# A four-layer transformer kernel: router scatters one step sooner, normalising ahead of the batch chains, clearing at step 0, expert weights ahead of rows

## The chip, the cores and the metric

The kernel is one program on one core of a Trainium2 chip. The metric is the time of one execution on the device, in microseconds. An effect below about 0.2% of it can't be told from no change.

## The reference

8192 tokens (128 sequences of 64) of width 128 go through four layers, each an attention to a context and a feed-forward part, both behind a layer norm and a gate:

```python
x = x + tanh(g_xattn[i]) * xattn_i(layernorm(x), ctx)
x = x + tanh(g_ffn[i]) * ffn_i(layernorm(x))
```

- Attention: 16 heads. Layer 0 has a key width of 64 per head (1024 in all), layers 1 to 3 of 8 (128 in all). Layer 2 has a mask, layer 3 uses stablemax in place of softmax.
- Feed-forward of layers 0 and 3: a top-1 mixture of 8 experts with a capacity of 1024 tokens each. `logits = x @ W`, the expert is the argmax, and a token's place in its expert is the running count of the tokens ahead of it that chose the same (`cumsum(onehot) - 1`); tokens past the capacity are dropped. The rows of each expert go through `act(X @ W1 + b1) @ W2 + b2`, 128 to 512 to 128.
- Feed-forward of layer 1: two quantised linear maps.
- Feed-forward of layer 2: a top-2 mixture of 8 experts, `silu(x @ Wg) * (x @ Wu) @ Wd`, without a capacity.

## The kernel before

Each engine (PE for matmuls, DVE for vectors, ACT for activations, POOL, and SP for DMAs) has its own program and runs in order; semaphores tie them. The code of an engine is a loop of steps; in step `t` an engine does stage `s` of item `t - s`, so that all stages of different items overlap. The program has these parts in a row: attention of layer 0 (`attention_wide`, one tile of 128 tokens per step, 64 steps), experts of layer 0, attention of layer 1 with its quantised feed-forward behind it in the same loop, attention of layer 2 (`attention_split`, two tiles per step, 32 steps), the middle experts, attention of layer 3 (`attention_split`), the last experts. In the trace the three `attention_split` are told apart by time; their tiles all have names with `l_`.

**The router.** The class `Router` (in the loops called `tail`) hangs behind the attention of layers 0, 2 and 3. For each item that the attention has finished it does, in stages counted from `T0` (8 in layer 0):

- DVE (`Router.dve`): `bn_stats` (L702), `bn_aggr` (L754) of the same item, and one step later `tensor_scalar` L759, which writes the normalised rows `xn` from the mean and from `rstd`.
- POOL: `add_eps` (L624, waits for the aggregate) and `root` (L629, a power), which give `rstd`.
- PE and ACT: transpose of the rows (L653), scores (L661). DVE copies the scores (L670).
- Per batch of `nb` steps two short chains of dependent small operations on DVE: the **choice** chain (L726 to L749), which picks the expert by maximum and comparison and writes `chosen`; PE counts who is ahead (L642 to L646); the **slots** chain (L709 to L719), which turns the counts into the row number `put` of each token. `nb` is 4 in layers 0 and 3 and 2 in layer 2. A step with the first chain is called a choice step below, one with the second a slots step. In layer 3 the slots step comes right behind the choice step.
- POOL (`Router.scatter`, L617): one indirect DMA per tile and choice writes the rows to `slots` in memory at the places `put`. That is 1 per step in layer 0, 4 in layer 2, 2 in layer 3. The first of a step waits for `put_done` and for the landing of the scatters of two steps before. The item that is sent in step `t` is that of stage `s + 4 + nb`: one step behind the one in which the slots chain of its batch runs.

**POOL's order.** In layer 0 a step is: attention's norms, `scatter`, `add_eps`, `root`. In layer 2 (`folded`): wait for `scored`, `scatter`, then L916 (epsilon for the attention's norm), L624, L921 (its power), L629. In layer 3 (`stable`): L916, L624, L921, L629, then `Head.combine` (L397 twice, L401, L403: the results of the middle experts are weighted and added to x), then a wait for `o_filled`, then `scatter`. POOL's aggregate of step `t` is that of DVE's step before.

**DVE's order in `attention_split`**, after L1026 and L670 of the step: L991 (`l_xn`, waits for POOL's L921), L978 and L982 (statistics of a later item; in layer 3 L978 waits for L403), L1039 and L1041 (context divided, which PE L1298 waits for), L966 (x updated), `Router.dve`, L1061 (a 128x1024 product). `prepare` (L950) clears `l_val`, `l_split`, `l_recip` and the router's tiles; PE's first L1239 waits for it (`ready`).

**Experts.** `experts` handles items of 512 rows. For the middle ones (`dynamic`) the row numbers and the expert of an item are read from tables. SP issues per step the rows of item `t` (L1789, two DMAs) and the first weights of item `t - 1` (L1797, two DMAs); PE transposes the rows (L1976) and multiplies (L1968).

Of the kernel before, what the change touches and what calls it, by code (L numbers as in the profile page):

```python
# [7 lines left out]
ALU = mybir.AluOpType  # L8
# [520 lines left out]
class Router:  # L529
# [58 lines left out]
    def depth(self):  # L588

        return 5 + self.nb  # L590
# [8 lines left out]
    def scatter(self, nc, pool, t, s):  # L599

        g, k = self.g, self.tiles
        out = s + 4 + self.nb
        sent_before = t.landed(out + 2, k * self.ks)

        slotted = t.batches(out - self.nb + 1 + (t.t - out) % self.nb, self.nb) if t.live(out) else None
        if t.live(out):

            if self.slots_clear and t.t == out:

                pool.wait_ge(*self.slots_clear)  # L610
            for tile in range(t.item(out) * k, t.item(out) * k + k):
                for c in range(self.ks):

                    if c == 0 and tile % k == 0:
                        wait(pool, self.put_done, slotted)
                        wait(pool, self.sent[t.par(out)], sent_before)
                    pool.indirect_dma_start(  # L617
                        self.slots, bass.IndirectOffsetOnAxis(ap=g.put[c][:, tile:tile + 1], axis=0), g.row[:, tile, self.sent_cols], None,
                        bounds_check=self.slots.shape[0] - 1, oob_is_err=False).then_inc(self.sent[t.par(out)], 16)
# [56 lines left out]
    def dve(self, nc, dve, t, s, updated, n_updated, read, n_read):  # L676
# [21 lines left out]
        if t.live(s):  # L698
# [4 lines left out]
            last.then_inc(self.part, 1)  # L703
        if batch4:
# [46 lines left out]
        if t.live(s):  # L751
            wait(dve, self.part, n0)
            for tile in range(k):
                last = V.bn_aggr(self.mv[:, t.par(s), tile, :], self.st[:, t.par(s), tile, :])  # L754
            last.then_inc(self.stats, 1)
        if t.live(s + 1):
            wait(dve, self.rstd_done, n1)
            for tile in range(k):
                last = V.tensor_scalar(  # L759
                    g.xn[:, t.item(s + 1) * k + tile, :], g.x[:, t.item(s + 1) * k + tile, :],  # L760
                    self.mv[:, t.par(s + 1), tile, 0:1], self.rstd[:, t.par(s + 1), tile:tile + 1], ALU.subtract, ALU.mult)
            last.then_inc(self.xn_done, 1)
# [16 lines left out]
def attention_split(nc, g, name, gate_col, kind, head=None, stream=None, router=None, together=None, weights=None, out=None, follow=None):  # L779
# [13 lines left out]
    with ExitStack() as ctx:  # L793
# [113 lines left out]
        def _(pool):  # L907
            def step(t):
                if folded:

                    wait(pool, scored, t.done(SCORE))
                    tail.scatter(nc, pool, t, T0)
# [15 lines left out]
                if stable:  # L928

                    wait(pool, o_filled, t.done(OUT))  # L930
                    tail.scatter(nc, pool, t, T0)
# [16 lines left out]
        def _(dve):  # L948
# [121 lines left out]
            for t in range(FOLLOW + follower.STEPS if follower else STEPS):  # L1070
                if t == 3:
# [294 lines left out]
def attention_wide(nc, g, t_in, router, dropped, later):  # L1366
# [7 lines left out]
    with ExitStack() as ctx:  # L1374
# [88 lines left out]
        def _(pool):  # L1463
            def step(t):
# [14 lines left out]
                tail.scatter(nc, pool, t, 8)  # L1479
                tail.add_eps(nc, pool, t, 8)  # L1480
                tail.root(nc, pool, t, 8)

# [219 lines left out]
def experts(nc, g, name, slots, rows, w1, b1, w2, b2, kind, gate_col, last=False, early=None):  # L1702
# [13 lines left out]
    with ExitStack() as ctx:  # L1716
# [55 lines left out]
        def _(sp):  # L1772
            def step(t):
# [8 lines left out]
                if t.live(0):  # L1782

                    wait(sp, xt_filled, n4)
# [6 lines left out]
                if t.live(1):  # L1791

                    wait(sp, h_filled[3], t.done(1 + WS))
                    if not dynamic:
                        wait(sp, h_drained[3], n3)
                    for h in range(HALVES):
                        sp.dma_start(w1_s[:, t.par(1, WS), h, :, :], at(w1_v, expert(sp, t, 1, h))).then_inc(w1_in[t.par(1, WS)], 16)  # L1797
                    if not dynamic:
                        sp.dma_start(b1_s[:, t.par(1), :], b1[bass.ds(expert(sp, t, 1, 0), 1)].rearrange("a f c -> (a f) c")).then_inc(
                            w1_in[t.par(1, WS)], 16)  # L1800
# [530 lines left out]
```

## Time and profile before

| | us |
|---|---|
| median of 3 runs | 2513.36 |
| lowest, highest | 2510.45, 2514.68 |
| the profiled execution | 2513.01 |
| its span | 2511.2 |

The span runs from the first to the last instruction; 1.8 us lie around it. The granted TensorE clock was 0.915 of full speed on the mean. Busy time of the engines by stage, in us:

| stage | from, to | PE | DVE | ACT | POOL |
|---|---|---|---|---|---|
| layer 0 attention | 0, 780 | 716 | 559 | 400 | 284 |
| layer 0 experts | 780, 922 | 125 | 70 | 42 | 68 |
| layer 1 | 922, 1375 | 354 | 373 | 368 | 184 |
| layer 2 attention | 1375, 1795 | 348 | 328 | 192 | 183 |
| middle experts | 1795, 2025 | 209 | 119 | 46 | 141 |
| layer 3 attention | 2025, 2368 | 273 | 274 | 261 | 237 |
| last experts | 2368, 2511 | 123 | 64 | 43 | 62 |

Over the span PE is busy 2146.8 us (85%), DVE 1787.9 (71%), ACT 1350.6 (54%), POOL 1157.7 (46%). DMA issues are not counted as busy time of SP. A busy engine in the table isn't a bound by itself: what counts is which one the others wait for, and that is read from the idle time in brackets at the end of a row in the timeline and from the releaser named beside it.

### The profile page before, as it was taken

What the parts mean: (1) busy time and instruction counts of PE and PEld (TensorE: products, weight loads), DVE (VectorE), ACT (ScalarE), POOL (GpSimd) and SP (SyncE); (2) the same over time, 40 slices, a digit from 0 to 9 for tenths busy, and PEclk for the clock granted to TensorE, in tenths of its full rate; (3) what the DMA queues carried; (4) which work ended last, traced back from release to release, by engine and by line L of the source; (5) the groups of instructions that cost most, each with busy time, mean ns of one, the idle gap of its engine ahead of it and who ended that gap; (6) DMA issues with size and microseconds to landing.
All of it is one profiled execution on the core that took longest, in us unless ns stands there. A gap on an engine that the chain in (4) does not pass through costs nothing. (4 is left out here: it accounts for less than half of the span.)

```text
span 2511.2 us, 81208 instructions
## 1 busy us (share of the span) xinstructions
PE 2146.8 (85%) x33432; PEld 1717.8 (68%) x33443; DVE 1787.9 (71%) x5105; ACT 1350.6 (54%) x2499; POOL 1157.7 (46%) x1712
## 2 busy tenths in 40 slices
PE   6999999999995969999555799998399958898597
PEld 5887878787874746777444577776399947777375
DVE  3777777777773648887896589886555559988354
ACT  3555555555551327886998455553122259979232
POOL 1333333434343541113776125555466666876444
PEclk8999999999997979998677899997699979989699
DMA  6330000000005621110000111111487622332363
GB/s 194 110 123 27 25 27 25 24 21 20 20 18 152 180 85 55 55 58 17 1 1 3 32 37 52 52 51 36 134 235 230 185 75 79 106 96 79 101 185 103
DMA packets 225233, 195.14 MB, mean 78 GB/s; under 512 B 34444, under 2 KB 197846, under 8 KB 224864
## 3 DMA queue, kind: packets, MB, share of 16 engines
q1 hardware_dynamic: 186336, 143.52, 19.6%
q0 software_dynamic: 18944, 36.98, 4.2%
q10 hardware_dynamic: 19584, 9.44, 1.3%
q8 instruction: 265, 4.34, 0.8%
q14 instruction: 104, 0.85, 0.1%
HBM read 113.53 MB, written 70.55 MB: 73 GB/s over the span
## 5 line engine op out<-in xcount | busy, mean ns | idle before, releaser
L617 POOL DMA_INDIRECT slots<-row,put x256 | 258.1, 1008 | 211.5 <-issue 131.2
L1968 PE MATMUL experts_H<-experts_xs_t,experts_w 128*128 128x256 f32 (+1 forms) x832 | 253.5, 456 | 9.9 <-DMA experts_w<-in_F_w 4.7
L1102 ACT ACTIVATE l_prob_t<-l_banks 128x512 f32<-128x512 f32 x256 | 132.2, 603 | 145.9 <-PE l_banks L1219 115.4
L1968 PEld LDWEIGHTS experts_H<-experts_xs_t,experts_w 128*128 128x128 f32 x832 | 156.7, 195 | 74.5 <-issue 54.0
L1474 POOL TENSOR_TENSOR l_var_eps<-l_mv,eps 128x1 f32<-128x1 f32 x64 | 12.1, 189 | 413.9 <-DVE l_mv L1555 413.9
L1277 PE MATMUL l_banks<-l_val,l_prob_t 128*64 128x18 f32 x5120 | 201.1, 215 | 0.0
L1277 PEld LDWEIGHTS l_banks<-l_val,l_prob_t 128*64 128x64 f32 x5120 | 190.3, 143 | 8.1 <-issue 0.7
L1510 DVE TENSOR_REDUCE l_top<-l_S 128x16 f32<-128x1024 f32 x64 | 78.3, 1224 | 161.7 <-PE l_S L1653 161.7
L1986 PE MATMUL experts_Y<-experts_w,experts_hid 128*128 128x128 f32 x1600 | 190.0, 275 | 3.5 <-DVE experts_y L1912 2.6
L1986 PEld LDWEIGHTS experts_Y<-experts_w,experts_hid 128*128 128x128 f32 x1600 | 184.3, 192 | 5.0 <-issue 4.9
L1823 POOL DMA_INDIRECT rows<-experts_y,experts_idx x144 | 139.9, 971 | 90.0 <-DVE experts_y L1908 52.9
L1012 DVE TENSOR_REDUCE l_top<-l_banks 128x32 f32<-128x2048 f32 x64 | 146.5, 2288 | 46.3 <-PE l_banks L1226 33.7
L916 POOL TENSOR_TENSOR l_var_eps<-l_mv,eps 128x2 f32<-128x2 f32 x96 | 24.3, 253 | 302.3 <-DVE l_mv L982 218.7
L1944 ACT ACTIVATE experts_hid<-experts_H,experts_b_scaled 128x512 f32<-128x512 f32 x128 | 80.0, 687 | 135.2 <-DVE experts_b_scaled L1864 115.7
L1619 PE MATMUL l_R<-l_ctx_t,l_wk 128*128 128x128 f32 x1024 | 134.2, 286 | 11.6 <-DMA l_ctx_t<-in_ctx_t 11.6
L1619 PEld LDWEIGHTS l_R<-l_ctx_t,l_wk 128*128 128x128 f32 x1024 | 122.5, 196 | 19.9 <-issue 18.3
L1469 POOL TENSOR_TENSOR l_prob<-l_prob,l_recip 128x1024 f32<-128x1024 f32 x64 | 121.3, 1895 | 24.6 <-DVE l_recip L1506 24.6
L1941 ACT ACTIVATE experts_act_gate<-experts_H 128x512 f32<-128x512 f32 x72 | 43.0, 597 | 163.3 <-PE experts_H L1968 163.3
L1567 ACT ACTIVATE l_q_t<-l_R 128x512 f32<-128x512 f32 x128 | 76.4, 597 | 96.9 <-PE l_R L1619 96.9
L1619 PE MATMUL l_R<-l_xn_t,l_wq 128*128 128x128 f32 x1024 | 126.5, 277 | 2.0 <-DVE l_xn_t L1527 2.0
L1690 PE MATMUL l_R<-l_wo,l_out_t 128*64 128x128 f32 x2048 | 126.1, 276 | 0.0
L1111 ACT ACTIVATE l_k_m<-l_banks,early_bk_masked,const_table 128x256 f32<-128x256 f32 x256 | 124.9, 595 | 0.0
(312 smaller groups left out, 5943.4 us busy)
## 6 DMA issues: line engine op xcount, KB each, us to landing
experts_w<-in_F_w SPq DMA_DIRECT2D x136, 256.0 KB
l_ctx_t<-in_ctx_t SPq DMA_DIRECT2D x96, 128.0 KB, 2.4
early_q_m<-l_q_t SPq DMA_DIRECT2D x384, 32.0 KB, 1.8
experts_xs<-slots SPq DMA_DIRECT2D x72, 132.0 KB
experts_w<-in_F_w ACTq DMA_DIRECT2D x72, 128.0 KB, 3.3
slots<-l_empty SPq DMA_DIRECT2D x16, 536.0 KB, 4.1
experts_xs<-slots SPq DMA_DIRECT2D x16, 536.0 KB
slots<-l_empty SPq DMA_DIRECT2D x16, 520.0 KB, 5.9
```

Source lines behind the costliest of these rows:

```text
L617: pool.indirect_dma_start(self.slots, bass.IndirectOffsetOnAxis(ap=g.put[c][:, tile:tile + 1], axis=0), g.row[:, tile, self.sent_cols], No ...
L1012: V.tensor_reduce(top[:, :, :].rearrange("p r a -> p (r a)"), X[:, :, :].rearrange("p r (a k) -> p (r a) k", k=64), AX.X, ALU.max).then_in ...
L1102: nc.scalar.activation(prob_t[:, t.par(PROB), r, :], Z[:, r, :], ACT.Exp).then_inc(prob_done, 1)
L1111: last = nc.scalar.activation(k_m[:, t.par(PROJ, SLOTS_QK), j, :], QK[:, 256:512], ACT.Identity, bias=bk_masked[:, j:j + 1], scale=g.const ...
L1277: last = nc.tensor.matmul(O[64 * tile:64 * tile + 64, 18 * h:18 * h + 18], term[:, t.par(OUT), h // 4, col:col + 64], val[:, t.par(OUT), t ...
L1469: nc.gpsimd.tensor_tensor(prob[:, t.par(5, 4), :, :, :], prob[:, t.par(5, 4), :, :, :], recip[:, t.par(5), :, :].unsqueeze(3).broadcast_to ...
L1619: last = nc.tensor.matmul(R[:, BANK[name], P * k:P * k + P], w[:, 4 * (c % 2) + k, :], moving, start=True, stop=True)
L1690: last = nc.tensor.matmul(MISC[64 * b:64 * b + 64, P:2 * P], out_t[:, t.par(7), k, b, :], wo_s[:, b, k, :], start=k == 0, stop=k == 7)
L1823: pool.indirect_dma_start(rows, bass.IndirectOffsetOnAxis(ap=idx[:, t.par(4, XS), k:k + 1], axis=0), y[:, t.par(4), k, :], None, bounds_ch ...
L1944: nc.scalar.activation(hid[:, t.par(2), c, :], H[:, c, :], ACT.Gelu if kind == "gelu" else ACT.Relu, bias=b1_scaled[:, t.par(2), c:c + 1], ...
L1968: last = nc.tensor.matmul(H[:, c, cols], w1_s[:, t.par(2, WS), h, c, :], xs_t[:, t.par(2), cols], start=True, stop=True)
L1986: last = nc.tensor.matmul(Y[:, P * k:P * k + P], hid[:, t.par(3), c, P * k:P * k + P], w2_s[:, t.par(3, WS), k // SUBS, c, :], start=c == ...
```

## The change

There are five edits.

1. `Router.depth` is `4 + nb` instead of `5 + nb`, and `scatter` sends the item of stage `s + 3 + nb` instead of `s + 4 + nb`, in layers 0, 2 and 3. The first item of a batch goes out in the step of its slots chain.
2. In `Router.dve`, L759 (now L707) and L754 (now L714) stand ahead of the slots chain and the choice chain, the normalising first.
3. In `attention_wide`, POOL's `scatter` stands behind `add_eps` and `root`; in layer 2 it stands at the end of POOL's step, with its wait for `scored`.
4. In `attention_split`, `prepare` runs at step 0 of DVE's loop instead of step 3, in layers 1, 2 and 3.
5. For the middle experts SP issues in step `t` the first weights of item `t`, then its rows. The weights' wait (`h_filled[3]` of four items before) now stands ahead of the rows. The other experts keep their order.

```diff
     def depth(self):
 
-        return 5 + self.nb
+        return 4 + self.nb
...
     def scatter(self, nc, pool, t, s):
 
         g, k = self.g, self.tiles
-        out = s + 4 + self.nb
+        out = s + 3 + self.nb
...
             last.then_inc(self.part, 1)
+        if t.live(s + 1):
+            wait(dve, self.rstd_done, n1)
+            for tile in range(k):
+                last = V.tensor_scalar(
+                    g.xn[:, t.item(s + 1) * k + tile, :], g.x[:, t.item(s + 1) * k + tile, :],
+                    self.mv[:, t.par(s + 1), tile, 0:1], self.rstd[:, t.par(s + 1), tile:tile + 1], ALU.subtract, ALU.mult)
+            last.then_inc(self.xn_done, 1)
+        if t.live(s):
+            wait(dve, self.part, n0)
+            for tile in range(k):
+                last = V.bn_aggr(self.mv[:, t.par(s), tile, :], self.st[:, t.par(s), tile, :])
+            last.then_inc(self.stats, 1)
         if batch4:
...
             last.then_inc(self.chosen_done, 1)
-        if t.live(s):
-            wait(dve, self.part, n0)
...
-            last.then_inc(self.stats, 1)
-        if t.live(s + 1):
-            wait(dve, self.rstd_done, n1)
...
-            last.then_inc(self.xn_done, 1)
...
             def step(t):
-                if folded:
-
-                    wait(pool, scored, t.done(SCORE))
-                    tail.scatter(nc, pool, t, T0)
                 if t.live(NORM):
...
                     wait(pool, o_filled, t.done(OUT))
                     tail.scatter(nc, pool, t, T0)
+                if folded:
+
+                    wait(pool, scored, t.done(SCORE))
+                    tail.scatter(nc, pool, t, T0)
...
-                if t == 3:
+                if t == 0:
                     prepare()
                     dve.wait_ge(ready, 1)
...
-                tail.scatter(nc, pool, t, 8)
                 tail.add_eps(nc, pool, t, 8)
                 tail.root(nc, pool, t, 8)
+                tail.scatter(nc, pool, t, 8)
...
+            def load_w1(t, s):
+
+                wait(sp, h_filled[3], t.done(s + WS))
+                for h in range(HALVES):
+                    sp.dma_start(w1_s[:, t.par(s, WS), h, :, :], at(w1_v, expert(sp, t, s, h))).then_inc(w1_in[t.par(s, WS)], 16)
+
...
                 if t.live(0):
 
+                    if dynamic:
+                        load_w1(t, 0)
                     wait(sp, xt_filled, n4)
...
-                if t.live(1):
-
-                    wait(sp, h_filled[3], t.done(1 + WS))
-                    if not dynamic:
-                        wait(sp, h_drained[3], n3)
-                    for h in range(HALVES):
-                        sp.dma_start(w1_s[:, t.par(1, WS), h, :, :], at(w1_v, expert(sp, t, 1, h))).then_inc(w1_in[t.par(1, WS)], 16)
...
+                if t.live(1) and not dynamic:
+                    wait(sp, h_drained[3], n3)
+                    load_w1(t, 1)
```

DVE, layer 3, a slots step, before (L702 and L754 are the router's statistics, L712 to L719 the chain that writes `put`, L759 the normalising, L1061 the attention's next work):

```order
3465 L702 BN_STATS l_tail_st<-row 128x6 x2
3466 L712 TENSOR_TENSOR l_cand<-l_hot,l_counts 128x64
3467 L713 TENSOR_REDUCE l_rank<-l_cand 128x8
3468 L716 TENSOR_SCALAR l_lost<-l_rank 128x8
3469 L717 TENSOR_TENSOR l_slot<-l_rank,l_expert_base 128x8
3470 L718 TENSOR_TENSOR l_rank<-l_slot,l_lost 128x8
3471 L719 CAST put<-l_rank 128x8
3472 L754 BN_AGGR l_tail_mv<-l_tail_st 128x2 x2
3473 L759 TENSOR_SCALAR row<-row,l_tail_mv,l_tail_rstd 128x128 x2
3474 L1061 TENSOR_TENSOR l_soft<-l_soft,l_prob_t 128x1024
```

and the same place in the changed kernel:

```order
3465 L702 BN_STATS l_tail_st<-row 128x6 x2
3466 L707 TENSOR_SCALAR row<-row,l_tail_mv,l_tail_rstd 128x128 x2
3467 L714 BN_AGGR l_tail_mv<-l_tail_st 128x2 x2
3468 L724 TENSOR_TENSOR l_cand<-l_hot,l_counts 128x64
3469 L725 TENSOR_REDUCE l_rank<-l_cand 128x8
3470 L728 TENSOR_SCALAR l_lost<-l_rank 128x8
3471 L729 TENSOR_TENSOR l_slot<-l_rank,l_expert_base 128x8
3472 L730 TENSOR_TENSOR l_rank<-l_slot,l_lost 128x8
3473 L731 CAST put<-l_rank 128x8
3474 L1061 TENSOR_TENSOR l_soft<-l_soft,l_prob_t 128x1024
```

The normalising and the aggregate moved ahead of the six rows of the chain; `put` is written two rows (four instructions) later. L1061 stays behind both.

POOL, layer 3, the place of the first scatters, before:

```order
1122 L403 TENSOR_TENSOR row<-row,l_term 128x2x128
1123 L916 TENSOR_TENSOR l_var_eps<-l_mv,eps 128x2
1124 L624 TENSOR_TENSOR l_tail_var_eps<-l_tail_mv,eps 128x2
1125 L921 TENSOR_TENSOR l_rstd<-l_var_eps,neg_half 128x2
1126 L629 TENSOR_TENSOR l_tail_rstd<-l_tail_var_eps,neg_half 128x2
1127 L397 TENSOR_TENSOR l_term<-l_got,weight 128x256 x2
1128 L401 TENSOR_TENSOR l_term<-l_term 128x256
1129 L403 TENSOR_TENSOR row<-row,l_term 128x2x128
1130 L617 DMA slots<-row,put 8192x268 x2
```

and in the changed kernel:

```order
1122 L403 TENSOR_TENSOR row<-row,l_term 128x2x128
1123 L617 DMA slots<-row,put 8192x268 x2
1124 L912 TENSOR_TENSOR l_var_eps<-l_mv,eps 128x2
1125 L624 TENSOR_TENSOR l_tail_var_eps<-l_tail_mv,eps 128x2
1126 L917 TENSOR_TENSOR l_rstd<-l_var_eps,neg_half 128x2
1127 L629 TENSOR_TENSOR l_tail_rstd<-l_tail_var_eps,neg_half 128x2
```

The first pair of a batch now stands one step sooner, ahead of the next step's norms and combine. In layer 2 POOL's rows stand in the same order in both kernels; what they wait for differs.

SP, the start of the middle experts, before (each DMA behind the load of its table entry):

```order
453 L1778 TENSOR_LOAD tile_row
...
456 L1789 DMA experts_xs<-slots 128x2x132
...
460 L1789 DMA experts_xs<-slots 128x2x132
...
464 L1789 DMA experts_xs<-slots 128x2x132
...
468 L1789 DMA experts_xs<-slots 128x2x132
...
472 L1797 DMA experts_w<-in_F_w 128x512
...
476 L1797 DMA experts_w<-in_F_w 128x512
```

and in the changed kernel:

```order
453 L1758 TENSOR_LOAD tile_expert
...
456 L1777 DMA experts_w<-in_F_w 128x512
...
460 L1777 DMA experts_w<-in_F_w 128x512
...
464 L1797 DMA experts_xs<-slots 128x2x132
...
468 L1797 DMA experts_xs<-slots 128x2x132
...
472 L1777 DMA experts_w<-in_F_w 128x512
...
476 L1777 DMA experts_w<-in_F_w 128x512
```

The weights of item 0 moved ahead of all rows, and those of item 1 ahead of the rows of item 1.

## Rows read from the trace of the kernel before

Of a row of the timeline: start in us, duration in us, engine, line, operation, output and inputs by name, and in brackets the idle time of the engine before it and what ended it.

**Rows 1.** Timeline, end of layer 0's attention: start us, us, engine, line, operation, [idle before]

```profile
764.58 0.45 PE L653 MATMUL l_R<-const_table,row 128*128 128x128 f32 x1 [2.27 <-DVE row L759]
```

**Rows 2.** Timeline, the first steps of layers 1, 2 and 3

```profile
924.99 0.37 ACT L1122 COPY l_xn_t<-l_banks 128x256 f32<-128x256 f32 x1 [21.73 <-PE l_banks L1253]
926.70 1.22 PE L1239 MATMUL l_banks<-l_ctx_t,early_wk 128*128 128x256 f32 x2 [1.75 <-DVE l_recip L957]
...
1382.12 0.54 DVE L953 MEMSET l_val<- 64x576 f32 x1
1382.84 0.37 ACT L1122 COPY l_xn_t<-l_banks 128x256 f32<-128x256 f32 x1 [5.43 <-PE l_banks L1253]
1383.87 1.22 PE L1239 MATMUL l_banks<-l_ctx_t,early_wk 128*128 128x256 f32 x2 [1.07 <-DVE l_recip L957]
...
2034.21 1.22 PE L1239 MATMUL l_banks<-l_ctx_t,early_wk 128*128 128x256 f32 x2 [3.31 <-DVE l_recip L957]
```

**Rows 3.** Timeline, one batch of layer 2 in full flow

```profile
1575.25 0.17 DVE L719 CAST put<-l_rank 128x4 uint32<-128x4 f32 x1
...
1576.28 1.04 POOL L617 DMA_INDIRECT slots<-row,put  x1 [5.65 <-issue]
...
1581.45 0.73 POOL L921 TENSOR_TENSOR l_rstd<-l_var_eps,neg_half 128x2 f32<-128x2 f32 x1
...
1584.47 0.59 DVE L991 TENSOR_SCALAR l_xn<-row,l_mv,l_rstd 128x128 f32<-128x128 f32 x2
```

**Rows 4.** Timeline, end of layer 2's attention

```profile
1755.89 0.60 DVE L759 TENSOR_SCALAR row<-row,l_tail_mv,l_tail_rstd 128x128 f32<-128x128 f32 x2 [1.69 <-POOL l_tail_rstd L629]
1756.04 1.10 POOL L617 DMA_INDIRECT slots<-row,put  x1 [0.19 <-issue]
...
1769.38 0.19 DVE L709 TENSOR_TENSOR l_ranked<-l_counts,l_slot_base 128x32 f32<-128x32 f32 x1
...
1770.23 0.96 POOL L617 DMA_INDIRECT slots<-row,put  x1 [1.86 <-issue]
...
1770.57 0.17 DVE L719 CAST put<-l_rank 128x4 uint32<-128x4 f32 x1
...
1788.48 0.97 POOL L617 DMA_INDIRECT slots<-row,put  x1 [0.30 <-issue]
```

**Rows 5.** Timeline, start of the middle experts

```profile
1791.94 3.88 SPq L1789 DMA_DIRECT2D experts_xs<-slots  x4
...
1796.59 1.46 SPq L1797 DMA_DIRECT2D experts_w<-in_F_w  x2
...
1801.28 1.19 PE L1968 MATMUL experts_H<-experts_xs_t,experts_w 128*128 128x256 f32 x2 [4.67 <-DMA experts_w<-in_F_w]
```

**Rows 6.** Timeline, layer 3: a choice step, the slots step behind it, a later step

```profile
2153.82 0.21 POOL L624 TENSOR_TENSOR l_tail_var_eps<-l_tail_mv,eps 128x2 f32<-128x2 f32 x1 [1.23 <-DVE l_tail_mv L754]
...
2157.89 1.57 DVE L991 TENSOR_SCALAR l_xn<-row,l_mv,l_rstd 128x128 f32<-128x128 f32 x2
...
2159.54 1.06 POOL L617 DMA_INDIRECT slots<-row,put  x1 [0.17 <-issue]
...
2162.67 0.17 DVE L719 CAST put<-l_rank 128x8 uint32<-128x8 f32 x1
...
2163.24 1.96 POOL L921 TENSOR_TENSOR l_rstd<-l_var_eps,neg_half 128x2 f32<-128x2 f32 x1
2163.40 1.22 DVE L1061 TENSOR_TENSOR l_soft<-l_soft,l_prob_t 128x1024 f32<-128x1024 f32 x1
...
2168.01 0.72 POOL L403 TENSOR_TENSOR row<-row,l_term 128x256 f32<-128x256 f32 x1
2168.77 0.49 DVE L978 BATCH_NORM_STATS2 l_st<-row 128x6 f32<-128x128 f32 x2 [0.75 <-POOL row L403]
...
2247.79 1.06 POOL L617 DMA_INDIRECT slots<-row,put  x1 [5.52 <-PE l_banks L1277]
```

**Rows 7.** Timeline, end of layer 3's attention

```profile
2355.03 0.97 POOL L617 DMA_INDIRECT slots<-row,put  x1 [0.30 <-issue]
```

More of the change, by code:

```diff
@@ L750, in dve @@
             last.then_inc(self.chosen_done, 1)
-        if t.live(s):
-            wait(dve, self.part, n0)
-            for tile in range(k):
-                last = V.bn_aggr(self.mv[:, t.par(s), tile, :], self.st[:, t.par(s), tile, :])
-            last.then_inc(self.stats, 1)
-        if t.live(s + 1):
-            wait(dve, self.rstd_done, n1)
[L758 to L761, printed above, removed]
-            last.then_inc(self.xn_done, 1)
     def chain(self, count, name):
@@ L1790, in step @@
                             x_in[t.par(0, XS)], 16)
-                if t.live(1):
-                    wait(sp, h_filled[3], t.done(1 + WS))
-                    if not dynamic:
-                        wait(sp, h_drained[3], n3)
-                    for h in range(HALVES):
-                        sp.dma_start(w1_s[:, t.par(1, WS), h, :, :], at(w1_v, expert(sp, t, 1, h))).then_inc(w1_in[t.par(1, WS)], 16)
-                    if not dynamic:
-                        sp.dma_start(b1_s[:, t.par(1), :], b1[bass.ds(expert(sp, t, 1, 0), 1)].rearrange("a f c -> (a f) c")).then_inc(
-                            w1_in[t.par(1, WS)], 16)
+                if t.live(1) and not dynamic:
+                    wait(sp, h_drained[3], n3)
+                    load_w1(t, 1)
+                    sp.dma_start(b1_s[:, t.par(1), :], b1[bass.ds(expert(sp, t, 1, 0), 1)].rearrange("a f c -> (a f) c")).then_inc(
+                        w1_in[t.par(1, WS)], 16)
                 if t.live(2) and not dynamic:
```

## Prediction

> **What bounds the kernel now.** The table of stages in the section on time and profile says that TensorE (PE) is busy 85% of the span. So an edit on another engine pays or costs only where PE is already waiting for it, and I read the timeline at those places: the start and the end of each attention, and one step of layer 3, the only loop in which GpSimd (POOL) is nearly as busy as PE. In the steps of layer 3, POOL's chain closes a loop: it scatters two tiles, computes two norms, combines rows, and its last row L403 releases VectorE (DVE) L978 after 0.75 us of idle [rows 6]. DVE then feeds PE. Whatever is put in front of L403 there makes the step longer. In layer 0 and layer 2 POOL has room: a 5.65 us gap stands in front of a scatter group of layer 2 [rows 3].
>
> **Sending one step sooner.** No scatter is added or removed; the first group of each batch is now issued in the step in which DVE writes `put`, so it waits for L719. The wait costs what `put` lags behind the point at which POOL is ready, plus the handover. Handover: in layer 2 `put` is written at 1575.42 (1575.25 + 0.17) and L617 starts at 1576.28, so 0.86 us [rows 3].
>
> Layer 3, slots step (one step in four): POOL reached L617 at 2159.54 and nothing held it. `put` of that step is ready at 2162.84 (2162.67 + 0.17) [rows 6]. The same change puts normalise and aggregate in front of the chain, some 0.65 us by the starts of such rows, so `put` comes at about 2163.49 and L617 at 2164.35. POOL is held for 4.81 us. From 2164.35 it needs 2.35 for the pair (two of about 1.06 and 0.97 with 0.3 between), 0.3 up to L921, and then what stands between L921 and the end of L403: 2168.73 - 2163.24 = 5.49 us [rows 6]. Of these 1.2 are no work: L921 takes 1.96 there and 0.73 where nothing is beside it [rows 3, 6], because DVE's L1061 ran beside it; delayed, it no longer meets L1061, so 4.26 are left. L403 ends at 2164.35 + 2.35 + 0.3 + 4.26 = 2171.25 instead of 2168.73: **+2.5 us**, and DVE L978, which was waiting for just this row, passes it all on. Layer 3 has eight such steps. The first two thirds of the layer also carry the combine with L403, which is done for the last ones; of the six that lie in that part I count four. One is covered, since POOL there waits 5.52 us for PE L1277 anyway [rows 6], and one has no combine behind it. 4 x 2.5 = +10. Bounds: 0, if DVE is late anyway (as it is in the covered one), and 5 x 2.6 = +13.
>
> Layer 2, steady: `put` comes 0.65 later, four scatters at 1.27 and the two norms follow, L921 ends at 1582.18 + 0.65 = 1582.83, and its reader L991 starts at 1584.47 [rows 3]. 1.6 us are left: 0, and if this cover is gone, +0.65 in each of 14 batches (+9). Layer 0, steady: one scatter per step, several microseconds of idle POOL beside a step that PE sets: 0.
>
> **Normalising ahead of the chains.** The work on DVE is the same, its order differs. *Layer 3, choice step*: L624 waited 1.23 us for the aggregate behind the choice chain [rows 6]; that wait goes. But DVE's L991 is as late as POOL there: it ends at 2159.46, stretched to 1.57 us [rows 6] beside POOL rows. What is left is the stretch, about 0.5 us in each of four steps: **-2** (bounds -5 and 0). *Layer 0, drain*: PE L653 waits 2.27 us for L759 [rows 1], whose place moves ahead of a slots or choice chain in three of the last steps (0.2, 0.3 and 0.7 us of chain): **-1.1** (bounds -3 and 0).
>
> *Layer 2, drain*: here POOL is the bound, scattering back to back to 1788.48 [rows 4]. Today a slots chain runs on DVE while L759 would have to wait for POOL's root (1.69 us of idle in front of it [rows 4]). With L759 in front, the chain waits as well: the root now stands behind four scatters that wait for `put`, and the next `put` stands behind the root. L759 ends at 1756.49 + 0.65 = 1757.14, a slots chain of 1.36 us (1769.38 to 1770.74) and the aggregate follow, `put` comes at 1758.6, and the group at 1759.4 instead of 1756.04 [rows 4]: +3.4 for the batch. At the next batch both a choice chain and a slots chain stand behind the L759 that waits, which I work out the same way as +5.1 when its group starts. Behind it nothing waits for DVE any more. The 1.86 us that POOL idles in the middle of that group [rows 4] may stay or be absorbed, so +3.1 to +5.1, and DVE's own weighing, which starts behind the last `put`, slips by up to +6.5. I take **+5**. *Layer 3, drain*: the same knot once. The group behind the last `put` started at 2355.03 [rows 7] and would start at about 2356.4: **+1.4** (0 to +3).
>
> **Clearing at the first step.** The memsets that prepare `l_val`, `l_split` and `l_recip` release PE's first L1239. *Layer 1*: what it needs else, `l_xn_t`, is there at 925.36 (924.99 + 0.37), and L1239 starts at 926.70, after 1.75 us of idle [rows 2]. DVE has nothing to do before the first x has landed, so early memsets are free: **-1.3**. *Layer 2*: x is there at once, and no idle stands in front. The memsets take 1.9 us from 1382.12, now in front of the first statistics instead of beside ACT and PE; `l_xn_t` would be ready at 1383.21 + 1.9 = 1385.1 and L1239 starts then instead of at 1383.87 [rows 2]: **+1.3**. *Layer 3*: PE waits 3.31 us for the memsets [rows 2], but the next steps are paced by POOL's combine, so the head start is given back within two steps: 0, bounded by -2.8 and 0.
>
> **Weights, then rows** (middle experts). SP issued four row loads in 3.88 us from 1791.94, then two weight loads in 1.46 from 1796.59, and PE L1968 waited 4.67 us for the weights [rows 5]. Now weights 0 go first (1791.94 to 1793.4), rows 0 follow by 1795.7, which is some 2.2 us later than before. Until now PE was done with the first transposes at 1796.61 (1801.28 - 4.67) and, with a copy of nearly 1 us, could have started L1968 near 1797.5; 2.2 later makes 1799.7 instead of 1801.28: **-1.6** (bounds -3 and 0). Later the rows queue behind a weight load that waits for `h_filled` of four items earlier; PE is the bound and rows are fetched ahead: 0.
>
> **Sum.** -1.1 (layer 0) -1.3 +1.3 (clearing) +5 (drain 2) -1.6 (weights) +10 -2 (layer 3) +1.4 (drain 3) = **+11.7 us**. The profiled execution took 2513.01 us, 0.35 below the median of the three runs, so I forecast 2513.4 + 11.7 = **2525 us**.
>
> **A rule against a row.** At 2163.24 POOL starts L921 and at 2163.40, while it runs, DVE starts L1061; L921 takes 1.96 and L1061 its 1.22 [rows 6]: POOL, which was first, pays. The Trainium skill says in "SBUF — State Buffer", section "SBUF: two separate sides", that DVE with two SBUF inputs and GpSimd share an exclusive lock: whichever starts first keeps it for the whole instruction and the other blocks. The length agrees (0.73 + 1.22 = 1.95), the winner doesn't, as far as starts in the trace are exact. By the rule DVE's short chain rows would wait for POOL's powers, which the change moves beside them.
>
> **Rivals.**
> *Absorbed (2515 us).* POOL's hold in the slots steps is covered, as in the step in which it waits 5.52 us for PE [rows 6]. For it: PE's clock falls at times, and then PE is late. Against: in most steps DVE idles exactly 0.75 for L403. Without the +10 the sum is +1.7; with half of drain 2, less.
> *It works as meant (2503 us), the other side.* Place: layer 3's choice and slots steps. POOL's waits for the aggregate (1.23 and about 1 us in eight steps) go, DVE's L991 follows at once, and the first group finds its `put`. It decides if `put` comes before POOL has finished L403, that is over 3 us earlier than today. Then -8, and -1.1 -1.3 -1.6 +1.3 with no cost in the drains: -10.7. Against: `put` moves later, not earlier.
> *Layer 2 pays too (2532 us).* If the 1.6 us cover is used up in most batches, +0.5 x 14 = +7 on top of the sum.
> *The lock decides (2530 us).* L921 (0.73 us) beside a chain holds DVE up in the four choice steps: the -2 becomes +3.
> *It doesn't do what it says* is true in part already: in layer 2 POOL's rows stand in the same order as before, with other waits only.
>
> **Chances.** Forecast (2519 to 2530) 0.53; absorbed (2509 to 2518) 0.20; as meant (2500 to 2508) 0.15; layer 2 pays, 0.07; the lock, 0.05. A measurement of this kernel can tell about 0.2%, 5 us, from no change. Faster 0.17, same 0.21, slower 0.62. The range goes down to 2507, leaving out most of the faster case, and up to 2535: both ends of the unknown costs in layer 3 and in drain 2 lie in it.
>
> **What would show it.** Right: in slots steps of layer 3 an idle of 3 to 5 us in front of the first L617, released by L719 (its new line), and L978 idle for L403 over 2 us; no idle over 0.3 in front of L624 in choice steps; layer 2's last scatter 3 to 6 us later after its stage's start; L1239 of layer 1 sooner by 1.3 and of layer 2 later by 1.3; L1968's first wait about 3 us. Wrong: L617 with no wait for `put`, or a later L403 with an unchanged period of the loop, which would say that DVE or PE sets it. The weakest term is the count of four exposed steps.

## The result, and the profile after

| | median us | runs | lowest, highest |
|---|---|---|---|
| before | 2511.9 | 4 | 2508.7, 2514.7 |
| after | 2543.6 | 4 | 2540.6, 2547.5 |

The changed kernel is slower: the ratio is 1.0139, with a 95% interval of 1.0116 to 1.0161. The medians are 31.7 us apart where 11.7 were forecast, and the median after lies 9 us beyond the upper end of the range. The direction was right, the size was not.

The profiled execution of after has a span of 2538.9 us, 27.7 more than before. Laid side by side by the same instructions in both traces (first transposes of each group of experts, L1039 of each attention step), the difference comes from these places:

| stretch | forecast | measured |
|---|---|---|
| start of the program | 0 | -2.0 |
| layer 0 and its experts | -1.1 | -1.0 |
| layer 1's start | -1.3 | -0.2 |
| layer 2's start and first 8 steps | +1.3 | +2.5 |
| rest of layer 2's steps | 0 | +0.6 |
| layer 2's drain and start of the middle experts | +5 - 1.6 | +3.9 |
| middle experts (35 items) | 0 | 0.0 |
| layer 3, steps 0 to 8, with its start | 0 | -0.3 |
| **layer 3, steps 8 to 31** | **+10 - 2** | **+22.4** |
| layer 3's drain | +1.4 | +1.7 |

(The first line is not the change: the kernels of the experiments that have nothing edited in layer 0 begin 1.6 to 3.0 us sooner than this profile of before, too.) Outside layer 3's loop each stretch behind the first holds within 1.3 us, and together they give +7.2 where +3.7 was forecast. The rest of this section is about that loop. Times between two L1039, in us, from both traces; steps 9, 13, 17, 21 and 25 are slots steps, the one ahead of each is a choice step:

```
step      8     9     10    | 12    13     14    | 16    17     18   | 20    21     22    | 24    25     26
before   9.89  9.28   8.83  | 9.91  9.36   8.44  | 9.90  9.37   9.20 | 9.97 13.29   9.29  | 9.90  9.36   9.11
after    9.33 12.08  10.15  | 9.50 12.09  13.30  | 8.92 11.92   9.20 | 8.99 11.91  10.22  | 9.51 12.07  13.30
```

Slots steps are longer by 2.7 us, as forecast (2.5), choice steps shorter by 0.4 to 1.0 (0.5). What was not forecast is the step **behind** a slots step. First the timeline of after, slots step 13 (columns as in the rows of before):

```profile
2170.73 0.17 DVE L731 CAST put<-l_rank 128x8 uint32<-128x8 f32 x1
2170.81 1.23 DVE L1061 TENSOR_TENSOR l_soft<-l_soft,l_prob_t 128x1024 f32<-128x1024 f32 x1
2171.74 1.23 POOL L617 DMA_INDIRECT slots<-row,put  x1 [6.18 <-issue]
...
2174.57 0.73 POOL L917 TENSOR_TENSOR l_rstd<-l_var_eps,neg_half 128x2 f32<-128x2 f32 x1
...
2177.99 0.72 POOL L403 TENSOR_TENSOR row<-row,l_term 128x256 f32<-128x256 f32 x1
2178.74 0.48 DVE L978 BATCH_NORM_STATS2 l_st<-row 128x6 f32<-128x128 f32 x2 [2.81 <-POOL row L403]
...
2180.36 0.66 PE L1298 MATMUL l_banks<-const_table,l_ctx_out 128*128 128x128 f32 x2 [4.02 <-DVE l_ctx_out L1041]
```

L731 is the old L719. `put` is ready at 2170.90, the scatter starts 0.84 us later, where 0.86 was taken from [rows 3], POOL has stood for 6.18 us, L917 no longer meets L1061 and takes 0.73 instead of 1.96 [rows 6], DVE waits 2.81 us for L403 instead of 0.75 [rows 6], and PE 4.02 us for DVE. All of this is the chain that the prediction laid out. The next two views show what it did not have: the same stretches by step (length, then busy us and instructions of PE, PEld, DVE, ACT, POOL, then the granted clock of PE as a share of full speed, DMA share, GB/s). Before, steps 13 and 14:

```profile
2160.09:2169.45 9.36, 7.58 (x151) 6.42 (x151) 8.37 (x29) 7.58 (x14) 7.78 (x11) 1.00 0.31 96
2169.45:2177.89 8.44, 7.51 (x151) 6.42 (x151) 7.55 (x23) 7.21 (x14) 7.21 (x10) 1.00 0.33 106
...
2233.74:2247.03 13.29, 12.37 (x147) 10.35 (x147) 8.93 (x30) 8.40 (x14) 7.09 (x10) 0.51 0.36 107
```

After, steps 13, 14 and 26:

```profile
2167.34:2179.43 12.09, 8.44 (x156) 6.95 (x155) 8.19 (x28) 10.15 (x15) 7.04 (x11) 1.00 0.39 116
2179.43:2192.73 13.30, 12.37 (x147) 10.37 (x147) 7.31 (x24) 8.15 (x13) 6.72 (x10) 0.50 0.25 79
...
2302.25:2315.55 13.30, 12.37 (x147) 10.36 (x147) 6.47 (x20) 8.15 (x13) 4.12 (x6) 0.50 0.13 42
```

Behind the 4 us in which PE stood still, its granted clock is 0.50, that is 1.2 in place of 2.4 GHz. The same matmuls then take 12.4 us instead of 7.5, and PE sets the length of the step, 13.3 us. Before had one such step in the loop, the covered slots step 21; after has two, and others at a clock in between (steps 10 and 22, of 10.15 and 10.22 us, at 0.70 and 0.69, and step 18, of 9.20 us, at 0.77).

The rows of the other terms, after: layer 1, layer 2 and layer 3 start without waiting for the memsets; in layer 2 the scatters stand back for `put` and end 4.84 us later than [rows 4]; PE's first L1971 (old L1968) waits 0.86 us instead of 4.67 [rows 5].

```profile
922.74 1.19 PE L1239 MATMUL l_banks<-l_ctx_t,early_wk 128*128 128x256 f32 x2 [0.51 <-issue]
...
1382.19 1.19 PE L1239 MATMUL l_banks<-l_ctx_t,early_wk 128*128 128x256 f32 x2 [0.51 <-issue]
...
1576.85 1.03 POOL L617 DMA_INDIRECT slots<-row,put  x1 [7.74 <-issue]
...
1756.40 0.60 DVE L707 TENSOR_SCALAR row<-row,l_tail_mv,l_tail_rstd 128x128 f32<-128x128 f32 x2 [0.78 <-POOL l_tail_rstd L629]
...
1759.26 1.03 POOL L617 DMA_INDIRECT slots<-row,put  x1 [2.90 <-issue]
...
1793.32 0.97 POOL L617 DMA_INDIRECT slots<-row,put  x1 [0.30 <-issue]
1796.79 1.50 SPq L1777 DMA_DIRECT2D experts_w<-in_F_w  x2
...
1805.30 6.36 PE L1971 MATMUL experts_H<-experts_xs_t,experts_w 128*128 128x256 f32 x16 [0.86 <-DVE experts_xs_t L1881]
...
2035.22 1.19 PE L1239 MATMUL l_banks<-l_ctx_t,early_wk 128*128 128x256 f32 x2 [0.55 <-ACT l_xn_t L1122]
```

### The profile page after: what moved, and what is told of

Its sections match the earlier page's. It is cut to its first block and busy times, and to the rows that moved or that the text cites. A ratio compares the mean times of both kernels' runs of the same rounds, so it can differ in the third digit from the quotient of the medians.

```text
span 2538.9 us, 81216 instructions
## 1 busy us (share of the span) xinstructions
PE 2164.2 (85%) x33443; PEld 1726.8 (68%) x33443; DVE 1776.2 (70%) x5105; ACT 1352.2 (53%) x2499; POOL 1146.8 (45%) x1712
## 5 line engine op out<-in xcount | busy, mean ns | idle before, releaser
L617 POOL DMA_INDIRECT slots<-row,put x256 | 259.7, 1015 | 266.3 <-issue 205.7
L1971 PE MATMUL experts_H<-experts_xs_t,experts_w 128*128 128x256 f32 (+1 forms) x832 | 252.6, 455 | 6.1 <-DVE experts_xs_t L1881 3.4
L1971 PEld LDWEIGHTS experts_H<-experts_xs_t,experts_w 128*128 128x128 f32 x832 | 156.1, 194 | 70.3 <-issue 48.6
```

Source lines behind the costliest of these rows:

```text
L617: pool.indirect_dma_start(self.slots, bass.IndirectOffsetOnAxis(ap=g.put[c][:, tile:tile + 1], axis=0), g.row[:, tile, self.sent_cols], No ...
L1971: last = nc.tensor.matmul(H[:, c, cols], w1_s[:, t.par(2, WS), h, c, :], xs_t[:, t.par(2), cols], start=True, stop=True)
```

## The experiments

Theory 1: in layer 3 POOL is held for `put`, and PE's clock falls behind the wait that this gives PE. Theory 2: the loss is the new order on DVE, or many small losses in all layers. Later theory 3: the sooner sending itself, by its transfers, does the harm. Ratios are against the kernel before in the same comparison, with 95% intervals. The 78 single executions of before in these comparisons lie between 2496 and 2527 us, so the totals tell some 5 us apart, and the traces tell more.

**The edits one by one.** Edits 1 and 3 alone:

```diff
-        return 5 + self.nb
+        return 4 + self.nb
...
-        out = s + 4 + self.nb
+        out = s + 3 + self.nb
...
-                tail.scatter(nc, pool, t, 8)
                 tail.add_eps(nc, pool, t, 8)
                 tail.root(nc, pool, t, 8)
+                tail.scatter(nc, pool, t, 8)
```

(and the same place of the scatter in layer 2 as in the change).

> Edits 1 and 3 alone (scatter one step sooner, POOL's place of it), DVE's order as before. Theory 1, POOL held for `put` in layer 3 plus the fall of PE's clock behind the longer idle: `put` comes 0.65 us sooner than with all edits, so each of six slots steps costs 1.9 to 2.1 us instead of 2.7 (+12), and one or two steps run at half clock for 4 to 5 us each: 2524 to 2536 us. Theory 2, the order on DVE (normalising and aggregate ahead of the chains) is the main cause: at most +8, that is under 2520 us.

Measured: 2537.3 us, ratio 1.0089 (1.0063 to 1.0115). In its trace layer 3's steps 8 to 31 take 24.2 us more than before, with slots steps of 11.9 us and the steps behind at 10.1 to 10.3 and once 13.3; everything else together 1.4 us. Theory 1 stands, 1.3 us above its range, and one of its numbers was wrong: the slots steps should have been 0.65 us shorter than in after, since `put` comes sooner, and they are shorter by at most 0.2. The trace of this kernel, step 17, says why:

```profile
2209.14 0.17 DVE L719 CAST put<-l_rank 128x8 uint32<-128x8 f32 x1
2209.86 1.22 DVE L1061 TENSOR_TENSOR l_soft<-l_soft,l_prob_t 128x1024 f32<-128x1024 f32 x1
2210.15 1.86 POOL L617 DMA_INDIRECT slots<-row,put  x1 [4.32 <-issue]
2212.32 0.97 POOL L617 DMA_INDIRECT slots<-row,put  x1 [0.30 <-issue]
```

The scatter starts 0.29 us into L1061 and takes 1.86 us instead of 1.06 [rows 6]. It ends 0.93 us behind the end of L1061, and so does the scatter of 1.23 us in after (2172.97, with L1061 done at 2172.04): what POOL gains at the wait it loses in its own instruction.

Edit 2 alone, as in the change:

> Edit 2 alone (normalising and aggregate ahead of the chains), scatters in their old step. Theory 1: `put` is late by 0.65 us but nobody waits for it, L624's waits in choice steps go: -6 to +2, 2506 to 2514 us. Theory 2: +15 or more, over 2526 us.

Measured: 2502.3 us, ratio 0.9963 (0.9935 to 0.9991). It is a **gain**, of about 9 us, and better than the range of theory 1. In layer 3 a choice step takes 8.9 instead of 9.9 us and the slots step behind it 8.6 instead of 9.4; the loop is 12.6 us shorter, some 4 of them because no step ran at half clock. Layer 2's drain and the start of the experts take 5.6 us more. So the first form of theory 2, which blames the order on DVE, falls.

Edit 4 alone (`if t == 0` in place of `if t == 3`) and edit 5 alone:

> Edit 4 alone (clearing at step 0). By the two traces: layer 1's start gains some 1 us and gives part of it back behind a stretch of lower clock, layer 2's start loses 3 us over the first steps and layer 3's nothing: +1 to +4, 2513 to 2516 us. If clearing were only worth what the idle in front of L1239 shows: -3 to 0. The trace of each start tells them apart, the total may not.

> Edit 5 alone (weights, then rows, in the middle experts). In the changed kernel layer 2's end and this start together gave +3.9 us, and PE's first L1968 no longer waits for the weights. Alone it should give -3 to -1 us, 2509 to 2512 us; if the rows queued behind the weights' wait cost something later, the period of 5.68 us per item would grow, and it didn't in the changed kernel.

Measured: 2513.1 us, ratio 1.0004 (0.9979 to 1.0030), and 2512.7 us, ratio 0.9998 (0.9974 to 1.0023). Neither can be told from no change; the first lies in its range, the second 0.7 us above it. Between the first L1039 of layer 1 and the first of layer 2 the trace of edit 4 has 4.0 us more than before; but of the kernels that touch nothing there, the traces have between 2.8 less (the run with the wait alone, below) and 6.4 more (the last one, below), and the granted clock in layer 1 differs between them. So what clearing costs there is read at its own place only, at L1239. From the drain of layer 2 to the second item of the experts edit 5 has 0.8 us less; its -1.6 is at best half there.

**Layer 3 alone has the loss.** All edits, but in layer 3 the old step:

```diff
-        return 4 + self.nb
+        return (4 if self.kind != "gated" else 5) + self.nb
...
-        out = s + 3 + self.nb
+        out = s + (3 if self.kind != "gated" else 4) + self.nb
```

> All five edits, but in layer 3 the scatters stay in their old step. Theory 1 (POOL held for `put` in layer 3's slots steps, PE's clock falling behind it): the whole loss of layer 3 goes and the gain of edit 2 there comes out, slots steps of about 8.6 us and choice steps of about 8.9 us: 30 to 37 us less than with all edits, 2507 to 2514 us. Theory 2 (losses spread over the layers, drain of layer 2 and starts above all): not under 2530 us.

Measured: 2508.9 us, ratio 0.9989 (0.9974 to 1.0004): as theory 1 has it, 35 us less than after, with slots steps of 8.6 us from step 13 on and choice steps of 8.9 to 9.1 us. The second form of theory 2, small losses in all layers, falls. And the counterpart, the kernel before with the scatters sooner in layers 0 and 2 only (the same two lines, without the other edits, and edit 3):

> Edits 1 and 3 in layers 0 and 2 alone. Theory 1: POOL has room there, nothing moves: within 3 us of the kernel before, 2507 to 2516 us. Theory 2 (the sooner sending costs in every layer): +8 us or more.

Measured: 2513.5 us, ratio 1.0018 (0.9994 to 1.0041). Behind the start of the program no stretch of its trace outside layer 3 differs from before by more than 1 us. Layer 3, where this kernel has nothing edited, takes 4.0 us less in steps 8 to 31: no step there happened to run at half clock. So the length of this loop can differ by 4 us between two traces without an edit in it.

**The wait without the sooner sending.** The kernel before, with one wait more in layer 3:

```diff
                     wait(pool, o_filled, t.done(OUT))
+                    ahead = T0 + 3 + tail.nb
+                    if t.live(ahead):
+                        wait(pool, tail.put_done, t.batches(ahead - tail.nb + 1 + (t.t - ahead) % tail.nb, tail.nb))
                     tail.scatter(nc, pool, t, T0)
```

> The kernel before, and in layer 3 POOL waits for `put` of the current step at the old place of the scatters; which rows are sent in which step stays. Theory 1: the wait alone is the cost, slots steps 11.9 us instead of 9.4 and the step behind 10.1 instead of 8.5 to 8.8, as with edits 1 and 3 alone: 2530 to 2540 us. Theory 3 (the earlier sending collides with other transfers or with DVE, the wait is harmless): 2511 to 2517 us.

Measured: 2542.3 us, ratio 1.0123 (1.0086 to 1.0160). The wait alone, with every row sent when it was sent before, costs as much as the change. In its trace, step 17 and the one behind:

```profile
2197.28 0.17 DVE L719 CAST put<-l_rank 128x8 uint32<-128x8 f32 x1
2198.30 1.86 POOL L617 DMA_INDIRECT slots<-row,put  x1 [4.32 <-DVE put L719]
...
2205.92 0.49 DVE L981 BATCH_NORM_STATS2 l_st<-row 128x6 f32<-128x128 f32 x2 [2.81 <-POOL row L403]
```
```profile
2194.70:2206.61 11.91, 9.22 (x151) 7.34 (x151) 8.05 (x30) 8.70 (x14) 7.67 (x11) 0.86 0.33 98
2206.61:2219.90 13.29, 12.37 (x147) 10.36 (x147) 7.40 (x23) 8.14 (x13) 7.08 (x10) 0.50 0.31 95
```

Theory 3 falls. The expected total was passed by 2 us, and the parts differ from the change: only four slots steps are held, and four steps of the loop run at half clock (13.29 us each) where before had one. Three of these four stand behind a PE wait of 2.7 us, not of 4.

**Is it the clock?** All edits, and PE kept at work in layer 3's slots steps while it would wait:

```diff
+                if stable and tail and (t.live(TURN) or t.live(PROB)) and tail.batch(t, T0 + 4):
+                    wait(pe, xv_drained, beats(t.t, TURN, XV_BEATS))
+                    for _ in range(12):
+                        nc.tensor.matmul(XV[:, 0:P], ident, ident, start=True, stop=True)
                 if turns(t):
```

> All five edits, and in layer 3's slots steps PE does 12 more transposes of 128 x 128 (some 2.5 us, into a part of the accumulators that nobody reads) where it would wait for L1041. Theory 1a (the clock falls because PE waits 4 us there): the hold stays, slots steps 12 us, but the step behind takes 8.5 instead of 10.2 and none takes 13.3: 10 to 16 us less than with all edits, 2528 to 2534 us. Theory 1b (the step behind is long because POOL and DVE are late, the clock is a by-product): the same as with all edits, 2540 to 2547 us, with steps of 10.2 us behind the slots steps at a full clock.

Measured: 2539.4 us, ratio 1.0102 (1.0065 to 1.0139), and the steps 8 to 28 of layer 3 are those of after to 0.1 us, the 10.1 and the two 13.3 included. The 12 matmuls took 1.9 us, waits of 2.1 to 2.7 us were left, and the clock fell all the same. This neither showed nor ruled out the clock, so the same with `range(26)`:

> As the run with 12 more transposes in layer 3's slots steps, but with 26, which fill the whole wait for L1041 (12 left 2.1 of 4.0 us idle, and the granted clock still fell to 0.50 behind it). Theory 1a (idle PE ahead of it makes the clock fall): no step at a clock of 0.5, the step behind the slots step 8.5 us, 8 to 16 us less than with all edits: 2528 to 2536 us. Theory 1b (the fall has another cause, or the long step is POOL's and DVE's): steps of 10.2 and 13.3 us as before, 2540 to 2547 us.

Measured: 2530.8 us, ratio 1.0087 (1.0061 to 1.0114). The steps 12, 13, 14, and 25, 26 of its trace:

```profile
2152.95:2162.38 9.43, 7.91 (x161) 6.70 (x161) 9.15 (x33) 9.07 (x14) 7.31 (x10) 1.00 0.37 108
2162.38:2174.99 12.61, 12.61 (x202) 11.71 (x200) 8.27 (x29) 6.44 (x12) 6.50 (x10) 1.00 0.23 71
2174.99:2183.91 8.92, 7.95 (x154) 6.65 (x154) 7.93 (x21) 8.82 (x16) 6.97 (x10) 1.00 0.36 106
2280.19:2292.80 12.61, 12.61 (x201) 11.71 (x200) 8.28 (x29) 6.98 (x12) 6.49 (x10) 1.00 0.17 53
2292.80:2301.40 8.60, 7.63 (x152) 6.42 (x151) 6.67 (x18) 8.53 (x15) 4.36 (x6) 1.00 0.26 80
```

Now PE is busy for the whole slots step, and the clock is 1.00 in all of steps 8 to 29. The five steps behind a slots step take 44.3 us together, where after has 56.2 and before 44.9. The hold itself stays, and the 26 matmuls overrun it by 0.5 to 0.7 us in each slots step, too little to give the 1.2 to 4.7 us that four of the steps behind are shorter than in after. So the fall of the clock follows from PE's wait in the slots step, and it is what makes the step behind long. In the totals this kernel is 21 us above before, the one with 12 matmuls 30 and the change 32; its interval overlaps that of the 12 matmuls and ends just below that of the change (1.0114 and 1.0116), so the verdict rests on the steps. Steps 8 to 26 as a whole, in before, in after, with the wait alone, with 12 matmuls and with 26:

```profile
2113.55:2293.57 180.02, 156.96 (x2913) 130.32 (x2911) 160.00 (x477) 153.61 (x246) 136.00 (x182) 0.92 0.31 94
```
```profile
2117.62:2315.55 197.93, 167.65 (x2914) 138.01 (x2913) 152.58 (x478) 156.33 (x248) 127.70 (x184) 0.85 0.29 88
```
```profile
2103.68:2308.76 205.08, 180.18 (x2913) 147.94 (x2911) 157.90 (x477) 155.87 (x248) 134.33 (x182) 0.80 0.27 84
```
```profile
2123.27:2321.09 197.82, 179.93 (x3034) 151.23 (x3033) 153.46 (x477) 156.32 (x248) 127.78 (x184) 0.86 0.29 89
```
```profile
2113.59:2301.40 187.81, 174.37 (x3174) 152.08 (x3173) 155.51 (x478) 153.81 (x247) 126.56 (x184) 1.00 0.31 92
```

No run shows which wait costs how much clock. In after, waits of 4.0 to 4.5 us are followed by 0.50 twice and by 0.69 to 0.77 three times; with the wait alone 2.7 us were enough for 0.50; and before has its one fall to 0.51 around a wait of 1.7 us, which left the clock at 1.00 in other steps. Nor does PE's idle time as a sum decide: it is 23 us in before and 18 us with 12 matmuls, at 0.92 and 0.86.

**What edit 2 gains.** Only the aggregate ahead of the chains (with edit 5), and only the normalising ahead:

> Only the aggregate stands ahead of the chains, in layers 0, 2 and 3; normalising stays behind them; edit 5 too. If POOL's wait for the aggregate (L624) was what edit 2 took away, this has the gain of edit 2 (-7 to -12 us) without the loss at the end of layer 2: 2495 to 2503 us. If normalising ahead brings the gain: 2508 to 2515 us.

> Only normalising stands ahead of the chains, the aggregate stays behind them. If the aggregate is the gain: no gain in layer 3's steps (choice steps 9.9, slots steps 9.4 or more), and the loss at the end of layer 2 (+5): 2514 to 2520 us. If normalising is the gain: 2500 to 2505 us.

Measured: 2507.6 us, ratio 0.9996 (0.9969 to 1.0023), and 2528.4 us, ratio 1.0075 (1.0044 to 1.0107). The mechanism is right in layer 3: with the aggregate alone a choice step takes 9.1 us and a slots step 8.8 in most batches, so 1.3 of the 1.7 us per batch come from it. With normalising alone they take 10.2 and 9.4, and the waits of POOL over steps 9 to 28 of layer 3 are (engine, line, waited for, us in total, times, longest), before, then with the aggregate alone, then with normalising alone:

```profile
POOL l_tail_var_eps L624 <- DVE l_tail_mv L754: 10.7, 10, 2.6
```
```profile
POOL l_tail_var_eps L624 <- DVE l_tail_mv L707: 1.6, 1, 1.6
```
```profile
POOL l_tail_var_eps L624 <- DVE l_tail_mv L761: 15.9, 11, 3.1
```

(L707 and L761 are the aggregate, ahead of the chain, and behind the chain and the normalising.) The stretch of L921 beside L1061 is not the gain: with normalising alone no power on POOL is stretched, and nothing is gained. The totals were missed in both. With the aggregate alone layer 0 takes 4.8 us more up to its experts: every step with a chain is 0.14 us longer, 32 times. Why is open: with edit 2 whole the same aggregate stands in front of the same chains, and the four steps of a batch take 45.7 us as before, where they take 45.9 here. With normalising alone the loss of 19 us is more than the 6 us by which its profiled execution is longer. That execution is its second fastest, at a granted clock of 0.917; the ten run from 2515 us at 0.918 to 2542 us at 0.902, so much of the rest goes with the clock. Which steps it falls in, no trace shows.

**A version that beats both.** Edit 2 in layers 0 and 3 alone, and edit 5, with the scatters in their old step:

```diff
+        if self.kind != "top2":
+            if t.live(s + 1):
+                wait(dve, self.rstd_done, n1)
...
+            if t.live(s):
+                wait(dve, self.part, n0)
...
         if batch4:
...
+        if not (self.kind != "top2"):
...
```

> Edit 2 in layers 0 and 3 alone, and edit 5. Edit 2 alone gave 2502 us and lost 5.6 us at the end of layer 2, where L707 stands ahead of the slots chain and waits for POOL's root. Without it there the loss goes: 2495 to 2500 us. If that loss was due to something else, 2502 us.

Measured: 2496.1 us, ratio 0.9948 (0.9921 to 0.9974): 0.5% faster than before and 1.9% faster than after, and in its range; from edit 2 alone (0.9963) its total can't be told. Layer 2's drain with the start of the experts takes 0.65 us less than before, not 5.6 more. Its steps 12 to 14 of layer 3:

```profile
2145.38:2154.34 8.96, 7.92 (x161) 6.70 (x160) 8.68 (x34) 8.59 (x14) 7.40 (x10) 1.00 0.36 107
2154.34:2162.92 8.58, 7.80 (x153) 6.45 (x152) 8.34 (x29) 7.77 (x14) 7.36 (x11) 1.00 0.37 107
2162.92:2171.41 8.49, 7.56 (x151) 6.42 (x151) 7.63 (x23) 8.04 (x14) 7.32 (x11) 1.00 0.39 115
```

Layer 3 keeps the full clock in steps 1 to 25; PE waits at most 1.1 us in the loop's steps there, 1.8 before.

## Why the prediction was right and wrong

**What bounds.** Right: the loss sits where POOL closes the loop, in layer 3, and nowhere that POOL has room. Edits 1 and 3 in layers 0 and 2 cost nothing that can be told, and in layer 2 L617 came 0.57 us later in full flow (1576.85, [rows 3]) with L991 where it was.

**The hold, 2.5 us.** Right in size and cause: +2.7 measured, with the handover at 0.84 (0.86 forecast), L917 back to 0.73, L978 waiting 2.81, and 6.97 us from the start of L617 to the end of L403 (6.90 forecast). POOL stood for 6.18 us, not 4.81: measured from the start of the step it got there 1.1 us sooner, and `put` came 0.8 us later, not 0.65. The count of exposed steps was wrong: five, not four. I took the fourth batch as covered, because POOL waited there 5.52 us for PE. That PE was late because its clock was at 0.51 in this one step. It was no property of the step, and in after the clock fell elsewhere. A cover that comes from a fall of the clock is not one.

**The step that failed: the clock stood at nothing.** The sum took PE's wait as lost time and nothing else. The rival named "absorbed" even says that PE's clock falls at times, and uses it only as a cover. It should have been a price. With PE's wait grown from at most 1.8 to 4.0 us and more, the five steps behind are longer than in before by 4.9, 4.2, 1.3, 0.9 and 0 us. The step to see it in was there, 13.29 us long at 0.51 where its neighbours take 8.4 to 10.0 us, and I read it as cover. The loop's +22.4 is +13.3 for five holds (steps 9, 13, 17, 21, 25, against 9.36 us for step 21) where the sum has +10 for four, -2.8 for four choice steps (-2), +11.3 for the steps behind (0), -3.9 for the slow step that before had and after hasn't (0), and +4.5 in the other steps (0). Most of the last is in steps 27 to 31, four of which ran at 0.64 to 0.86, where before had 0.73 to 1.00; how much of it is the clock wasn't told apart.

**Edit 2.** In the choice step -0.5 was forecast and -0.4 to -1.0 measured. But only the edit alone shows its worth, 1.7 us per batch: in the change the half that falls into the slots step is covered by the hold. By the terms of the sum edit 2 by itself would have been a loss of 3.3 us (-1.1 +5 -2 +1.4), where it is a gain of 9.

**The lock.** That rival had 0.05, and nothing came of it: the choice steps got shorter. What I overlooked is that the scatter is also a POOL instruction that can be stretched, by 0.8 us. Beside L1061, which kept 1.18 to 1.26 us, a scatter that started while it ran was stretched and ended 0.91 to 0.94 us behind it in every trace that has such a pair, and one that started ahead of it kept 0.97 to 1.07 us. The starts don't decide in every pair, though: L921 started 0.16 us ahead of L1061 and took 1.94 to 1.97, and of DVE's L991 and POOL's L403 it is DVE that is stretched, 0.88 us for 0.34 with a start 0.07 us ahead of L403.

**The drains.** Layer 2: 1759.4 forecast for the held group, 1759.26 measured; the last scatter +4.84 for +5. This is the term that was worked out from the order and it held to 0.2 us. It belongs to edit 2 alone: edits 1 and 3 alone move nothing there, and with edit 2 alone, whose scatters are in their old step, the held group has the same wait as in after. The root stood behind four scatters in before, too.

```profile
1752.36 1.03 POOL L617 DMA_INDIRECT slots<-row,put  x1 [2.90 <-issue]
```

Layer 3: +1.7 for +1.4. The weights: the wait of L1968 is 0.86 us and not the 3 us that was named as a sign, since PE's transposes now begin at 1803.36 (1795.53 before) and L1971 1.9 us behind them (5.8 before). From layer 2's last scatter to that first product there are 12.0 us instead of 12.8, in after and with edit 5 alone: -0.8, half of the -1.6.

**The starts.** At L1239 itself they were right: about -1 us in layer 1 (-1.3 forecast) and about +1.5 in layer 2 (+1.3), each against the lead that the trace of after had just ahead of it. But most of layer 1's gain was gone by the first L1039, behind two steps in which PE's matmuls ran at a lower clock (L1193 1.93 us for 1.07) where before has one, and a microsecond there can't be told from the clock.

**Rivals.** "As meant" failed at its own condition, `put` before L403's end. "Absorbed" had 0.20 and did not happen at all. The upper end of the range was too low because the clock was not in it.

## What to carry to other kernels

A wait added on an engine that closes the loop of a pipeline costs time in every round that meets it, even when the work behind it is only sent away. The cost is its length less the slack and the overlaps that it removes: here POOL stood 6.18 us and a step lost 2.7. Work out when the awaited thing is ready and when the waiter gets there, and if the second comes first by microseconds, leave the step of distance in. Price the idle time of TensorE twice, once for the wait and once for the clock of the step behind it (here 0 to 4.9 us a time), and don't count a slow step of the old profile as cover. When a change bundles edits, time the parts: here one of five was worth a gain of 0.4%, and its loss in layer 2's drain could be left out; both were buried under another edit.

## What was not expected of the hardware

- Behind 4.0 us of idle PE, the granted clock fell to 0.50 for a whole step, and it did so still behind 2.1 us of idle with 1.9 us of matmuls put ahead of it; with PE busy throughout the slots step it stayed at 1.00. In the kernel before, waits of 1.7 to 1.8 us stand beside a clock of 1.00 in some steps, of 0.81 in others and of 0.51 in one.
- An indirect DMA's issue on POOL takes 1.06 us, and 1.86 us when it starts 0.29 us into a DVE operation of 1.22 us with two SBUF inputs (L1061); it then ends 0.93 us behind that operation. Started ahead of it, it keeps 0.97 to 1.07 us.
- The handover from a DVE write of `put` to the start of the indirect DMA on POOL that waits for it is 0.83 to 0.86 us in 12 or more cases of every trace, with single cases between 0.78 and 1.17.
